# A fused adapter, attention and mixture-of-experts kernel: a plan in 32-bit words, two expert tiles fewer, and small VectorE passes merged, dropped or given to ScalarE

## The reference

```
dg, db, ug, ub = cond @ down_gamma, cond @ down_beta, cond @ up_gamma, cond @ up_beta
w_down = down_project * dg + db ;  w_up = up_project * ug + ub                      # one of each per sequence
h0 = relu(x @ w_down) @ w_up + x                                                     # conditional adapter
qkv = rmsnorm(h0) @ qkv_w + qkv_b                        # 16 query heads, 4 key heads, head size 64
q, k = rope(q), rope(k)
logits = q k^T / 8, causal, a learned sink logit per head in the denominator
x1 = h0 + softmax_with_sink(logits) v @ proj_w + proj_b
h2 = rmsnorm(x1)
glogits = h2 @ gate_w + gate_b                           # 32 experts
topv, topi = top_k(glogits, 4) ;  gw = softmax(topv)
y2 = sum over the 4 chosen experts e of  gw_e * (silu(h2 @ Wg_e) * (h2 @ Wu_e)) @ W_down_e
out = x + x1 + y2
```

## Time and profile before

| | us |
|---|---|
| median of 3 runs | 1040.16 (1039.16 to 1040.64) |
| the profiled execution, whole | 1039.19 |
| its span in the trace | 1037.4 |
| TensorE matmuls busy | 895.6 (86%) |
| VectorE busy | 804.4 (78%) |
| GpSimd busy | 550.4 (53%) |
| ScalarE busy | 512.5 (49%) |
| DMA, mean over the span | 243 GB/s |

### The profile page before, as it was taken

How to read it: one execution, slowest core, us unless ns; L and a number is a source line. 1 busy time by engine, 2 the same in 40 slices (tenths; PEclk the granted TensorE clock), 3 DMA queues, 4 the chain that set the end, 5 groups by cost and what they waited for, 6 DMA issues and landing times.

```text
span 1037.4 us, 21388 instructions
## 1 busy us (share of the span) xinstructions
PE 895.6 (86%) x7240; PEld 728.6 (70%) x7272; DVE 804.4 (78%) x1877; ACT 512.5 (49%) x1193; POOL 550.4 (53%) x513
## 2 busy tenths in 40 slices
PE   3859898997899989888851599999999999999985
PEld 2537676675676767567640488888888888888864
DVE  3878799898888889887755377777777777777777
ACT  1223463736445363553751366665665666566631
POOL 2436557877868687887778034333333333333440
PEclk8769999999899999999995699999999999999998
DMA  7235869687796977869875977778677758663589
GB/s 223 61 95 179 267 234 269 212 286 245 243 283 206 291 249 253 271 224 292 306 246 206 336 261 270 277 237 282 238 239 263 257 184 306 227 219 103 189 334 349
DMA packets 127683, 251.93 MB, mean 243 GB/s; under 512 B 18706, under 2 KB 66327, under 8 KB 127002
## 3 DMA queue, kind: packets, MB, share of 16 engines
q1 hardware_dynamic: 83866, 187.59, 54.8%
q0 software_dynamic: 13872, 34.64, 9.2%
q10 hardware_dynamic: 29840, 28.34, 8.8%
HBM read 136.19 MB, written 102.66 MB: 230 GB/s over the span
## 4 chain that ended last, share of the span: by engine, by line
PE 49%; POOL 12%; DMA 12%; DVE 11%; issue 7%; ACT 4%; SPq 4%; ACTq 0%; DVEq 0%; POOLq 0%
PE gbank L971 10%; PE scores L971 10%; POOL lists L673 7%; PE gbank L990 5%; PE scores L990 5%; DMA w_parts<-ring 4%; DMA ring<-in_W_up 3%; PE gbank L762 3%; DMA rows_in<-lists 3%; POOL ring L680 3%; PE gbank L843 3%; PE scores L945 2%; DVE ring L1402 2%; PE gbank L980 2%; PE gbank L945 2%
## 5 line engine op out<-in xcount | busy, mean ns | idle before, releaser
L695 POOL DMA_INDIRECT pick_rows<-rows_out,pair_i x161 | 160.7, 998 | 277.3 <-ACT rows_out L1233 268.5
L680 POOL TENSOR_TENSOR ring<-ring 128x512 fp32r<-128x512 f32 x96 | 123.2, 1296 | 47.3 <-ACT ring L1168 46.6
L971 PE MATMUL scores<-ring,in_part 128*128 x486 | 135.9, 415 | 0.0
L971 PE MATMUL gbank<-ring,in_part 128*128 x480 | 131.8, 409 | 0.0
L673 POOL DMA_INDIRECT lists<-put_rows,slot_i x104 | 101.5, 976 | 49.9 <-issue 27.3
L762 PE MATMUL gbank<-h_t,w_qk 128*128 128x512 f32 x480 | 122.0, 407 | 7.0 <-DVE h_t L1389 4.7
L843 PE MATMUL gbank<-w_o,ring 128*128 128x256 f32 x512 | 118.3, 385 | 3.8 <-ACT ring L1114 3.7
L1402 DVE SCALAR_TENSOR_TENSOR ring<-gbank,b_qk,rope 128x512 f32<-128x512 f32 x160 | 109.9, 744 | 14.7 <-PE gbank L762 14.1
L762 PEld LDWEIGHTS gbank<-h_t,w_qk 128*128 128x128 f32 x480 | 89.6, 191 | 32.2 <-issue 8.6
L843 PEld LDWEIGHTS gbank<-w_o,ring 128*128 128x128 f32 x512 | 96.2, 193 | 17.3 <-ACT ring L1114 5.2
L1168 ACT ACTIVATE ring<-ring 128x512 fp32r<-128x512 f32 x96 | 59.9, 628 | 92.2 <-DMA w_parts<-ring 49.1
(11 more groups left out here) (200 smaller groups left out, 1879.2 us busy)
## 6 DMA issues: line engine op xcount, KB each, us to landing
w_parts<-ring SPq DMA_DIRECT2D x192, 256.0 KB, 3.3
ring<-w_parts SPq DMA_DIRECT2D x32, 1536.0 KB, 7.6
rows_in<-lists ACTq DMA_DIRECT2D x161, 136.0 KB, 4.0
ring<-in_W_up SPq DMA_DIRECT2D x64, 256.0 KB, 3.5
picks<-pick_rows SPq DMA_DIRECT2D x8, 2048.0 KB, 11.9
ring<-in_W_down SPq DMA_DIRECT2D x32, 256.0 KB, 4.0
q_r<-rot SPq DMA_DIRECT2D x16, 512.0 KB, 6.8
q_r<-ring SPq DMA_DIRECT2D x16, 512.0 KB, 6.5
```

The source lines that it names most:

```text
L680: e.tensor_tensor(lower, lower.bitcast(F32), upper.bitcast(F32), ALU.subtract).then_inc(s_lower, 1)
L695: e.indirect_dma_start(out=pick_rows, out_offset=bass.IndirectOffsetOnAxis(ap=pair_i[:, i:i + 1], axis=0), in_=rows_out[i % NY][:, :], in_ ...
L971: ins = e.matmul(front[i % FRONTS], in_parts[i % IN_BUFS][x][:, c, :], ring[:, bass.ds(at + y * WE + c * 2 * DFF, 2 * DFF)], start=k == 0, ...
```

## The change

Seven edits:
- `AHEAD` goes from 3 to 1, so `NET` from 161 to 159; one fixed tile instead of three, two `fill_rows` DMAs fewer.
- `plan_wait` becomes int32. TensorE's sequencer masks the loaded number with 63 before it waits against it, once a tile.
- `softmax_a` on VectorE: the maximum with 0 is made inside the subtraction, `max(rowmax, 0) - score`; ScalarE's exponential gets the scale -1 and makes `st` itself with a Relu, waited for by its second exponential.
- `route_pick`: for groups of 4 tiles the four small multiply-adds become one multiplication and one addition of 128x128.
- `route_pick`: the cast of the top indices to float is left out; the comparison reads the unsigned integers.
- `route_list`: the pair's number and the rms factor are written by ScalarE in `root2` instead of VectorE.
- One more small constant (`pair_begin`) is loaded at the start.

```diff
-AHEAD = 3
+AHEAD = 1
 NET = PAIRS // P + E - 1 + (AHEAD - 1)
...
-    plan_wait = sb("plan_wait", [1, 2 * P], U16)
+    plan_wait = sb("plan_wait", [1, 2 * P], I32)
...
-                slot_of[i] = (slots[i // BATCH][i % BATCH], readies[i // BATCH][i % BATCH])
+                slot_of[i] = (slots[i // BATCH][i % BATCH], readies[i // BATCH][i % BATCH] & 63)
...
             e.activation(rms2[m % 2][:, lo:hi], ssq[m % 2][:, lo:hi], ACT.Exp, scale=-0.5).then_inc(s_rms2, 1)
+            w.wait_ge(s_late, LATE)
+            w.wait_ge(s_memset, ONES)
+            w.wait_ge(s_rms2, r + 1)
...
+            e.activation(entry[pb][:, at, 0], pair_no[:, at], ACT.Identity, bias=pair_begin[:, r:r + 1])
+            e.activation(entry[pb][:, at, 2].rearrange("p (s k) -> p s k", k=TOPK),
+                         rms2[m % 2][:, lo:hi].unsqueeze(2).to_broadcast([P, hi - lo, TOPK]), ACT.Copy).then_inc(s_entry, 1)
...
-            e.activation(score_view(t), score_view(t), ACT.Exp).then_inc(s_exp, 1)
+            e.activation(score_view(t), score_view(t), ACT.Exp, scale=-1.0).then_inc(s_exp, 1)
+            e.activation(st[:, 0, :], two[:, 0, :, 0], ACT.Relu).then_inc(s_top, 1)
+            w.wait_ge(s_top, t + 1)
             e.activation(two[:, 1, :, 1], st[:, 0, :], ACT.Exp, scale=-1.0).then_inc(s_sinkexp, 1)
...
-            top_or_sink = own.mark(e.tensor_reduce(st[:, 0, :], two[:, 0, :, :], axis=AX.X, op=ALU.max))
-            w.wait_ge(s_vector, top_or_sink)
-            e.tensor_tensor(score_view(t), score_view(t), st[:, 0, :].unsqueeze(2).to_broadcast([P, 16, T]),
-                            ALU.subtract).then_inc(s_shift, 1)
+            e.scalar_tensor_tensor(out=score_view(t), in0=two[:, 0, :, 0].unsqueeze(2).to_broadcast([P, 16, T]), scalar=0.0,
+                                   in1=score_view(t), op0=ALU.max, op1=ALU.subtract).then_inc(s_shift, 1)
...
+            if n > 2:
+                scaled = own.mark(e.tensor_tensor(glog[:, 0:n, :], gbank[banks[0]][:, 0:n * E].rearrange("p (s n) -> p s n", n=E),
+                                                  rms2[m % 2][:, lo:hi].unsqueeze(2).to_broadcast([P, n, E]), ALU.mult))
+                w.wait_ge(s_vector, scaled)
+                e.tensor_tensor(glog[:, 0:n, :], glog[:, 0:n, :], b_gate[:, :].unsqueeze(1).to_broadcast([P, n, E]),
+                                ALU.add).then_inc(s_glog, 1)
...
-            which = own.mark(e.tensor_copy(top_f[:, 0:n, :], top_i[:, 0:n, 0:TOPK]))
-            w.wait_ge(s_vector, which)
...
-            e.tensor_copy(entry[pb][:, at, 2].rearrange("p (s k) -> p s k", k=TOPK),
-                          rms2[m % 2][:, lo:hi].unsqueeze(2).to_broadcast([P, n, TOPK]))
-            e.tensor_scalar(entry[pb][:, at, 0], pair_no[:, at], float(TOPK * P * (TPM * m + lo)), None, ALU.add)
```

More of the change, by code:

```diff
@@ L10 @@
 F32, I32, U32, BF16 = mybir.dt.float32, mybir.dt.int32, mybir.dt.uint32, mybir.dt.bfloat16
-U16 = mybir.dt.uint16
 F32R = mybir.dt.float32r
@@ L283, in program @@
     pair_no = sb1("pair_no", [P, TPM * TOPK])
+    pair_begin = sb1("pair_begin", [P, GROUPS])
     x0_t = [sb1(f"x0_t{i}", [P, KC, MT]) for i in range(2)]
@@ L316, in program @@
     top_i = sb1("top_i", [P, TPM, 8], U32)
-    top_f = sb1("top_f", [P, TPM, TOPK])
     gexp = sb1("gexp", [P, TPM, TOPK])
@@ L428, in program @@
     s_sum, s_summed = sem("s_sum"), sem("s_summed")
+    s_entry, s_top = sem("s_entry"), sem("s_top")
     s_act_upper, s_up_upper, s_up_split = sem("s_act_upper"), sem("s_up_upper"), sem("s_up_split")
@@ L460, in program @@
         (b_gate[:, :], d["b_gate"]), (earlier_f[:, :], d["earlier"]), (expert_no[:, :], d["expert_no"]),
-        (list_base[:, :], d["list_begin"]), (filled[:, :], d["list_base"]), (pair_no[:, :], d["pair_no"]),
+        (list_base[:, :], d["list_begin"]), (filled[:, :], d["list_base"]), (pair_no[:, :], d["pair_no"]), (pair_begin[:, :], d["pair_begin"]),
         (tile_no[:, :], d["tile_no"]), (begun_slot[:, :], d["begun_slot"]),
@@ L1078, in root2 @@
             e.activation(rms2[m % 2][:, lo:hi], ssq[m % 2][:, lo:hi], ACT.Exp, scale=-0.5).then_inc(s_rms2, 1)
+            w.wait_ge(s_late, LATE)
+            w.wait_ge(s_memset, ONES)
+            w.wait_ge(s_rms2, r + 1)
+            pb, at = r % NPAY, slice(0, (hi - lo) * TOPK)
+            if r >= NPAY:
+                m0, _, hi0 = ROOTS[r - NPAY]
+                w.wait_ge(s_tagged, TPM * m0 + hi0)
+            e.activation(entry[pb][:, at, 0], pair_no[:, at], ACT.Identity, bias=pair_begin[:, r:r + 1])
+            e.activation(entry[pb][:, at, 2].rearrange("p (s k) -> p s k", k=TOPK),
+                         rms2[m % 2][:, lo:hi].unsqueeze(2).to_broadcast([P, hi - lo, TOPK]), ACT.Copy).then_inc(s_entry, 1)
         def norm1_sums(m, banks):
@@ L1159, in tag @@
             w.wait_ge(s_slot_i, r + 1)
+            w.wait_ge(s_entry, r + 1)
             e.activation(put_rows[put_at[t]][:, :, D:D + 4], entry[r % NPAY][:, s * TOPK:(s + 1) * TOPK, :],
@@ L1455, in route_pick @@
             w.wait_ge(s_rms2, r + 1)
[L1457 to L1461, removed]
+            if n > 2:
[4 more added lines that the diff above has]
+                                ALU.add).then_inc(s_glog, 1)
+            else:
+                for s in range(n):
+                    ins = e.scalar_tensor_tensor(
+                        out=glog[:, s, :], in0=gbank[banks[0]][:, s * E:(s + 1) * E],
+                        scalar=rms2[m % 2][:, lo + s:lo + s + 1], in1=b_gate[:, :], op0=ALU.mult, op1=ALU.add)
+                ins.then_inc(s_glog, 1)
             w.wait_ge(s_glog, r + 1)
@@ L1470, in route_pick @@
             w.wait_ge(s_vector, which)
-            which = own.mark(e.tensor_copy(top_f[:, 0:n, :], top_i[:, 0:n, 0:TOPK]))
-            w.wait_ge(s_vector, which)
             hot = own.mark(e.tensor_tensor(
-                onehot[:, 0:n * TOPK, :], expert_no[:, :].unsqueeze(1).to_broadcast([P, n * TOPK, E]),
-                top_f[:, 0:n, :].rearrange("p s k -> p (s k)").unsqueeze(2).to_broadcast([P, n * TOPK, E]), ALU.is_equal))
+                onehot[:, 0:n * TOPK, :].rearrange("p (s k) n -> p s k n", k=TOPK),
+                expert_no[:, :].unsqueeze(1).unsqueeze(1).to_broadcast([P, n, TOPK, E]),
+                top_i[:, 0:n, 0:TOPK].unsqueeze(3).to_broadcast([P, n, TOPK, E]), ALU.is_equal))
             w.wait_ge(s_vector, hot)
@@ L1742, in _constants @@
                     + np.arange(TOPK)[None, None, :]).reshape(P, TPM * TOPK).astype(f),
+        "pair_begin": np.tile(np.array([TOPK * P * (TPM * m + lo) for m, lo, _ in ROOTS], f), (P, 1)),
         "list_begin": np.tile(np.arange(E, dtype=f) * LIST + P + P * (np.arange(E) < AHEAD), (P, 1)).astype(f),
```

## The result

The changed kernel took 1033.00 us (median of 9 runs, 1029.66 to 1037.04), the kernel before 1040.52 in the same comparison (9 runs). The ratio is 0.9926, 95% interval 0.9905 to 0.9947: 7.5 us faster. The forecast of 1028.2 was 4.8 us too low. 1033.0 lies inside the whole range (1021 to 1035), but outside the 1024 to 1032 that I gave for the main case, and next to the rival of the slow load (1033.7). Two of the signs by which I meant to see that the forecast is wrong are there too: a period above 2.53, and a last list scatter that moved by more than 4 us. So the number alone can't tell which account holds; the traces and the experiments have to.

The account below looks back on a forecast made before the run. TensorE's matmuls were taken to bound stage two, with no engine full in stage one. Terms -5.1 -6.4 +0.6 -0.6 +1.0 -1.5 summed to -12.0 us, giving 1028.2 us at the median's level, range 1021 to 1035.

Parts of the forecast that it names:

- the main case: Whole kernel: all terms arrive as summed, 1028.2 us, own range 1024 to 1032; chance 0.58.
- the rival of the slow load: Stage two: the `plan_wait` load stays at 2 us, 5.5 us come back, 1033.7 us; chance 0.13.
- a period above 2.53: Stage two: a time per tile over 2.53 us would show the forecast wrong.
- a last list scatter that moved by more than 4 us: End of stage one: expected about 1.5 us sooner; a move above 4 us would show the forecast wrong.
- Two tiles fewer: Stage two, TensorE full: two tiles with dropped results go, 2 x 2.53 us, so -5.1 us.
- The 32-bit plan: Stage two: `plan_wait` load falls from 2.01 to 0.6 us, issue holes -5.5, last load -0.9; together -6.4 us.
- The mask: Stage two, between the transposes: one register instruction for 158 tiles, hidden under queued matmuls, 0 us.
- The rival on the other side: Stage two, between the transposes: the mask's register instruction drains TensorE's queue, costing up to 22 us; chance 0.06.
- The period kept at 2.53: Stage two: 159 tiles were expected to keep the old period of 2.53 us each.
- The start: Start of stage two: rows of tiles 1 and 2 load about 1 us later, 1.8 us of room; +0.6 us.
- The small passes: Stage one: VectorE's relief of 10 to 18 us worth 1.5 to 2.7, ScalarE's 12.5 us cost 0.9; taken as -1.5 us.
- The end: End of stage two and gathering: last row wait gone, -0.6 us; last scatters land amid parts 3 to 5, +1.0 us.

Follow-up runs that it names:

- the gap: 64 unused bytes per partition ahead of `rows_in`, in the kernel before with 159 tiles, 32-bit plan and mask but no small-pass edits: 1030.98 us; in the changed kernel: 1031.65 us.
- the doses: Changed kernel with work added in stage one's softmax: VectorE's row maximum made twice, 1042.13 us; separately, ScalarE's Relu with its wait made five times, 1039.63 us.

## Why the prediction was right or wrong

*Two tiles fewer, -5.1.* Right within what can be told, as far as the tiles themselves go. From the loads of parts to VectorE's first sum the kernel gained 6.8, for which I had 5.1, the last `plan_wait` load's 0.9 and the last row wait's 0.6. The tiles alone gave 3.9 us by the medians, in a kernel that also paid 2.1 for the moved addresses. On top of the 32-bit plan they gave next to nothing until the gap gave the addresses back (1033.3, 1033.2, then 1030.98).

*The 32-bit plan, -6.4.* The mechanism was right, at every step that could be seen: the load at 0.592, no issue wait before L990, the last load gone. The holes shrank by 4.6 us instead of 5.5, as the waits for rows rose from 1.1 to 1.6. In the ten executions with the fast load these waits lie between 0.6 and 3.5 us, in the four with the slow one between 0.6 and 1.1; that TensorE gets to the rows sooner because it no longer pauses fits this, and was not tried. Alone, with the mask, the plan gave 6.9 us by the medians and 5.9 by the ratio. One reading in my reasoning was off: the load of 2.07 us that began at 723.9 left 1.02 us of idle before 726.15, so the queue had covered 1.2 us of it, not 1.4 to 2. A load of 0.59 is covered either way. The rival of the slow load is out, though its number, 1033.7, came closer than mine. The Trainium skill's floor of some 600 ns for a load ("DMA: Bandwidth & Descriptors", section "Latency and other measured facts") agrees with 0.592. Its 200 ns a register ("Runtime: NRT & Kernel Launch", section "Instruction fetch mechanics") is stated for registers that the runtime loads from device memory, and does not describe eight 32-bit registers from SBUF; the 16-bit load's 2.01 us, 251 ns a register, is nearer to it. Between the two tables here, the width decides.

*The mask, 0.* Right. 32 ns a tile, below the 46 I had taken, and hidden: the undisturbed period with it is 2.529, as without it. The rival on the other side is out.

*The period kept at 2.53.* This step failed, by assumption: I multiplied the old period by 159 tiles and named the longer period only as a sign that something was wrong. Removing two tiles shortened two tables and moved the operands by 64 bytes, which cost 2.1 us. This is the largest single error of the sum.

*The start, +0.6.* From the last scatter to tile 3 nothing changed (17.92, 17.90). Tile 1's rows landed 0.2 us later behind the scatter (13.19, 13.40), not 1, and the 1.8 us of room held. The +0.5 of the first period is the place of the clock's rise, so that this stretch came out near +0.6 is luck. Over all executions, the second L980 begins 22.6 us behind the last scatter in the four with AHEAD at 3 and 23.2 in the ten with 1, and either kind spreads over 2 us or more: no start cost can be told from that.

*The small passes, -1.5.* The sign was open in the prediction, and the time could not settle it: 1.0002 alone, with an interval of about 2.6 us to either side. By the ratios no pair of runs shows a gain, so I take the term as 0, give or take some 2 us. What was wrong in the working can be said in part. VectorE's relief was 8.9 us of busy time, under my 10 to 18, since neighbouring passes took over the blocked time; the new L1471 alone has 7 x 0.49 = 3.4 us over L1468. The shares of the chain are a weak price: VectorE's read 11% of the whole in the kernel before, 10 in the one with the small passes alone and 7 in the changed one, and the doses gave 24% of the added work for VectorE and about 28% for ScalarE, where I had 15 and 7. At these prices 8.9 us of relief is worth -2.1 and ScalarE's 10.8 us cost +3.0, which would cancel. But that carries the price of a large dose over to a small amount, and the chain of the changed kernel does not show such a cost on ScalarE. A smaller relief than I took, with ScalarE nearly free, explains the runs as well. Which of the two holds stays open. On the blocked time the Trainium skill's rule for passes with two inputs in SBUF ("SBUF — State Buffer", section "Who interferes with whom") agrees: the addition with both inputs in SBUF, L1471, averages 767 ns, the multiplication from PSUM beside it, L1468, 280.

*The end, -0.6 and +1.0.* Right in both: the last row wait is gone, and the gathering took 1.0 us more, as it does in all the kernels with 159 tiles.

The 4.8 us between 1028.2 and 1033.0 are thus: the period 2.1, which is shown; the smaller gain in holes 0.9, read from one pair of executions; the small passes about 1.5, which no run separates from noise; and some 0.3 that the medians can't tell. So the mechanisms of the tiles, the load and the gathering were right, and the step that failed is the fixed period. The 5.8 us by which stage one was longer in the profiled execution are mostly not the change: last scatters of the same program parts lie 5 us apart from execution to execution.

## What to carry to other kernels

When an edit changes the size of any buffer, compare the addresses of the operands of the busiest loop before and after, and compare its undisturbed period, not its total: a gain elsewhere hides a loss of half a per cent per turn. A share of the chain in one execution is a poor price for work on an engine whose queue others wait behind. A dose of several times the amount, on each of the two engines, shows what is on the chain at that size; look at the chain of the kernel without the dose before carrying its price over to a smaller amount. Values that a sequencer loads from a table in a hot loop should be laid out as 32-bit words.

## What the hardware showed that I had not expected

Eight registers from 32-bit words took 0.59 us in the median and from 16-bit words 1.92 at the least, in every kernel of the study. The run with the 32-bit plan and its mask alone changed nothing else at the load. A register operation in front of a matmul took 32 ns and cost nothing while matmuls were queued.

The place of the buffers in SBUF changed the tile period of a loop that only TensorE bounds by 0.5 to 0.9% (2.529 to 2.543 and 2.552), at clock 1.00, with the same instructions. Best was `mid_part` and what lies behind it at 64 modulo 128; 0 and 32 were worse. The 64 in itself may be chance: `ring`, the moving operand, lay at 0 modulo 128 in all of them, and no run moved it.

In a stage where no engine was full, 24% of the 39 us added to VectorE and about 28% of the 28 us added to ScalarE came out as time, each within some 3 us.
